# Moving the gates' and picked sums' instructions of six background tails to other steps of a one-core transformer layer

## The reference

```
cluster_gates = _calibrate(xf @ cluster_sigs.T, knots, temperature)     # 8 clusters
cluster_idx   = argmax(cluster_gates)
tile_gates    = _calibrate(xf @ sigs.T, knots, temperature)             # 64 tiles
sel_gates     = the 8 tile gates of the picked cluster
tile_idx      = cluster_idx * 8 + argmax(sel_gates)
...
y = xf + mag(tile_idx) * directions[tile_idx] * output_scale            # then a layer norm
```

## Time and profile before

| | |
|---|---|
| median of 3 runs | 1847.26 us (1846.22 to 1847.81) |
| the profiled execution, its own time | 1845.4 us |
| its span | 1843.6 us |
| TensorE busy | 1751.8 us, 95% of the span |
| VectorE busy | 1158.2 us, 63% |
| ScalarE busy | 1146.2 us, 62% |
| GpSimd busy | 891.7 us, 48% |

### The profile page before, as it was taken

How to read it: one execution, slowest core, us unless ns; L and a number is a source line. 1 busy time by engine, 2 the same in 40 slices (tenths; PEclk the granted TensorE clock), 3 DMA queues, 4 the chain that set the end, 5 groups by cost and what they waited for, 6 DMA issues and landing times.

```text
span 1843.6 us, 27558 instructions
## 1 busy us (share of the span) xinstructions
PE 1751.8 (95%) x9204; PEld 849.1 (46%) x9204; DVE 1158.2 (63%) x2783; ACT 1146.2 (62%) x1554; POOL 891.7 (48%) x811
## 2 busy tenths in 40 slices
PE   5899999999999899999999999999999999999994
PEld 3444454454544445444554445445454444544452
DVE  5465546657476674847657576574756767385767
ACT  3567756666567664666656765666647676566653
POOL 2435535545545454555545354455654555544620
PEclk9899999999999999999999999999999999999997
DMA  5200000100200000010110000001020001000000
GB/s 163 51 13 1 1 12 1 24 13 1 69 1 13 1 12 12 1 35 1 47 24 1 13 1 24 1 1 35 1 58 1 2 1 24 12 1 1 1 12 12
DMA packets 96606, 32.32 MB, mean 18 GB/s; under 512 B 76304, under 2 KB 90704, under 8 KB 96464
## 3 DMA queue, kind: packets, MB, share of 16 engines
q1 hardware_dynamic: 96464, 30.56, 7.9%
HBM read 13.48 MB, written 4.19 MB: 10 GB/s over the span
## 4 chain that ended last, share of the span: by engine, by line
PE 80%; ACT 8%; DVE 7%; issue 4%; POOL 1%; DMA 0%; ACTq 0%; DVEq 0%; SPq 0%; POOLq 0%
PE attended L1295 22%; PE key_scores L1276 21%; PE misc L1205 7%; PE max_scores L1254 6%; PE misc L1335 6%; PE misc L1375 3%; PE misc L1305 3%; ACT relu L1653 2%; ACT probs L1662 2%; PE misc L1366 2%; PE misc L1439 1%; DVE relu L1939 1%; PE misc L1428 1%; PE misc L1210 1%; PE misc L1417 1%
## 5 line engine op out<-in xcount | busy, mean ns | idle before, releaser
L1662 ACT ACTIVATE probs<-key_scores 128x1024 f32<-128x1024 f32 x512 | 524.0, 1023 | 463.7 <-PE key_scores L1276 388.9
L2434 POOL TENSOR_TENSOR prob_sum<-prob_sum,probs 128x512 f32<-128x512 f32 x383 | 491.5, 1283 | 135.7 <-ACT probs L1662 111.7
L1295 PE MATMUL attended<-probs,values 128*64 128x512 f32 x2048 | 556.8, 616 | 0.1
L1939 DVE CUSTOM_DVE_ANT_0 relu<-max_scores,relu 128x512 f32<-128x512 f32 x508 | 330.1, 687 | 258.4 <-PE max_scores L1254 257.4
L1276 PE MATMUL key_scores<-q_high,k_chain 64*128 64x512 f32 x2048 | 459.0, 444 | 17.1 <-ACT probs L1662 16.1
L1276 PEld LDWEIGHTS key_scores<-q_high,k_chain 64*128 64x128 f32 x2048 | 192.2, 184 | 457.4 <-ACT probs L1662 220.6
L1959 DVE TENSOR_TENSOR running_sum<-running_sum,probs 128x512 f32<-128x512 f32 x384 | 266.3, 694 | 10.1 <-ACT probs L1662 3.2
L1653 ACT ACTIVATE relu<-max_scores 128x1024 f32<-128x1024 f32 x254 | 259.0, 1020 | 16.7 <-PE max_scores L1254 10.8
L2430 POOL TENSOR_TENSOR prob_sum<-probs 128x512 f32<-128x512 f32 x64 | 82.0, 1281 | 359.8 <-PE misc L1305 351.8
L1254 PE MATMUL max_scores<-k_max,q_high 64*128 64x512 f32 x1016 | 210.1, 410 | 21.5 <-DVE row_max L1939 13.2
L1276 PE MATMUL key_scores<-q_low,k_chain 64*128 64x512 f32 x1024 | 203.3, 393 | 0.0
(11 more groups left out here) (435 smaller groups left out, 1928.5 us busy)
## 6 DMA issues: line engine op xcount, KB each, us to landing
k_chain<-k_chain SPq DMA_DIRECT2D x32, 256.0 KB, 3.7
shift_row<-row_max SPq DMA_DIRECT2D x512, 0.5 KB, 2.0
buf_a<-in_x SPq DMA_DIRECT2D x8, 512.0 KB, 4.0
k_max<-k_max SPq DMA_DIRECT2D x16, 256.0 KB, 3.4
x_in<-in_x SPq DMA_DIRECT2D x7, 512.0 KB, 4.7
out_x<-buf_b SPq DMA_DIRECT2D x7, 512.0 KB, 3.1
heads_out<-in_qkv_wT SPq DMA_DIRECT2D x1, 1536.0 KB, 10.0
wo<-in_o_wT SPq DMA_DIRECT2D x1, 1024.0 KB, 6.3
```

The costliest lines, as they stand in the source:

```text
L1295: tensor.matmul(attended[head * HD:(head + 1) * HD, :], values_of(b, g // 2)[:, kt, g % 2 * HD:(g % 2 + 1) * HD], prob_slot(u, kt, head), ...
L1662: scalar.activation(probs[(u * KT + kt) % len(probs)][:, :, :], key_scores[:, :, :], ACT.Exp).then_inc(S["exp"])
L1939: vector.tensor_tensor_reduce(out=relu_of(u, i)[:, head, :], in0=max_area(u, i)[:, head, :], in1=relu_of(u, i)[:, head, :], scale=1.0, sca ...
L2434: gpsimd.tensor_tensor(prob_sum[1][:, :], prob_sum[1][:, :], probabilities, ALU.add).then_inc(S["prob_sum1"])
```

## The change

In `calibration`, `cal_b` waits for a step with room, for tails 0 to 5. In `tail`, the GpSimd product `pick_tiles` is put into the same step as the first `first_max`, and `tile_scores`, with the `cal_a` of the second calibration behind it, waits for a step with room, for tails 0 to 5 again (`FIRST_HALF` is 7).

```diff
@@ calibration
     plan.put("cal_a", j, which)
     yield EARLY
     plan.put("cal_exp", j, which)
-    yield LATE
+    yield ROOM if j < FIRST_HALF - 1 else LATE
     plan.put("cal_b", j, which)
```

## The result

| | before | after |
|---|---|---|
| median of 6 runs on one chip | 1847.31 us (1842.73 to 1847.81) | 1852.09 us (1848.78 to 1854.66) |
| after over before | | 1.0034, 95% interval 1.0023 to 1.0044 |
| the profiled execution, its span | 1843.6 us | 1847.0 us |

The kernel became slower, by 0.34% or 6.3 us by the ratio, with 4.2 to 8.1 as its interval (the medians of these few runs differ by 4.8). The prediction was 1847.0 us with a range up to 1851.2 and 0.76 on no change: wrong in sign, and the measured median lies 0.9 us above the range.

The account below looks back on a forecast made before the run. PE, busy 95% of the span, was taken to bound the kernel, so only its waits could shrink. Terms -3.3 - 0.6 - 0.7 + 3.3 + 1.0 = -0.3 us gave 1847.0 us, range 1842.6 to 1851.2.

Parts of the forecast that it names:

- Tails 1 and 3, the wait goes: PE's 1.63 us wait for row maxima in tails 1 and 3 nearly goes, -3.3 us for both.
- Tails 0, 2 and 4, nothing: Moving the picked sums and `cal_a` out of step 114 and its like saves 0, as PE has no wait there.
- preparation of chunks 5 and 7: Preparation moved to step 181 makes PE wait 1.6 us against 1.93 before, twice: -0.6 us, bounds -3.9 and +5.
- First norm: Tails 1, 3, 5, one step later: waits of 1.4 us against 0.36 at steps 140 and 141, three times, +3.3 us.
- Preparation of chunks 4 and 6: Steps 161 to 164: the second norm pair behind `inv` costs 0.6 us against 0.93 before, twice, -0.7 us.
- Tail 5: Second norm to first maximum, two steps later, takes the phase of tail 1: +1.0 us, bounds -1.1 and +2.
- the signs: Expected in the profile after: no `row_max` wait over 0.3 us at steps 177, 305, 431; stated waits at 140, 141, 183.
- GpSimd's queue: `pick_tiles` moves ahead of one running add, which slips about 1.3 us in tails 1 and 3; covered by buffers, 0.
- The port contention: GpSimd instructions lock ports shared with VectorE; so `cal_b` is stretched in chunks 5 and 7's new step, sum -0.3, else -0.9.
- the preparation lands behind GpSimd: Slower rival: `x_stats` starts 2.6 us later, PE waits 4.2; +4.6 for both chunks, 1852.2 us, chance 0.13.
- The later start is free: Faster rival: the losses at the first norm and in tail 5 go, only gains stay; -5.7, 1841.6 us, chance 0.17.
- the change doesn't do what it says: Rival: maxima of step 176 stay late because `first_max` ends late; -3.3 becomes 0, 1850.3 us, chance 0.05.

Follow-up runs that it names:

- e4: The changed kernel, but only the picked sums wait for a step with room, `cal_b` does not; 1847.1 us, ratio 1.0000 to the kernel before.
- e6: The kernel before with `pick_tiles` put with the first maximum in all tails, and tails 1, 3 and 5 started one step later; 1851.9 us, ratio 1.0027.
- e9: The changed kernel with ScalarE's `k_high` of each batch's last half-block of keys one step later; 1850.52 us, ratio 1.0018 to the kernel before.
- e13: e6 with the edit of e9, `k_high` one step later; 1845.2 us, ratio 0.9992 to the kernel before.
- e7: The changed kernel with the preparations of chunks 5 and 7 (and 3) asked for two units later; 1843.95 us, ratio 0.9984 to the kernel before.
- e10: The changed kernel with `pick_tiles` put back behind the wait for a step with room; 1854.28 us, ratio 1.0037 to the kernel before.
- e3: The changed kernel with the waits for room in tails 1 and 3 alone; 1845.87 us, ratio 0.9997 to the kernel before.
- e5: e4 with room for the picked sums in tails 1 and 3 alone; 1839.06 us, ratio 0.9961 to the kernel before.

## Why the prediction was wrong, step by step

**Tails 1 and 3, the wait goes: right.** -1.63 each, the maxima right behind the running sum.

**Tails 0, 2 and 4, nothing: nearly.** No wait came; the stretches are 1.3 us shorter together, by a cause left open. e4 shows the danger there that the step did not name: it weighed `cal_b` only as something that fits between maxima "as it did", and in step 116 it does not.

**A missing step: what the two delays do at steps 133 and 134.** "With tails 1, 3 and 5 one step later" was priced at the first norm only, and `x3` of tails 0, 2 and 4, which goes two steps later with the second calibration, had no term at all. The late start takes a 3.72 us output product from its place between T133 and T134, and that product was the cover of ScalarE's 2.30 us wait for `k_diff`: e6, with nothing but the late start, has 1.57 us of wait there. `x3`, put ahead of the maxima of step 132 and stretched, makes VectorE late: e9 keeps 1.05 us by that alone. 3 times 1.34 = +4.0 us, priced at 0; e13 has neither chain and no wait. The cover's own row was in the trace of before; I had costed the SP queue and the residual's bias at this place, and not asked which long product hid what.

**The term that was furthest off: preparation of chunks 5 and 7, mis-sized, with a wait missed.** -0.6 was predicted, +6.1 measured, 6.7 us off, where the whole sum is 6.5 off; all the rest, the +4.0 above included, nearly cancels. Its start came 3.32 us after T181, not 2.45 to 2.9: GpSimd's four products ran from 0.32 to 2.68, not to 2.2. The way from there to the scores is 4.84, as long as before; the 0.6 taken off it for the absent `q_high` was not to be had. So 2.62 of wait, not 1.6. Then came two things that no term had: 1.35 for the misc bank two steps on, and the lower clock behind the long wait, some 1.2 us in step 183 alone (6.60 against 5.43 in e9 with the same wait) and 1.5 in the stretch. The clock makes 2.9 of the 6.1 us, and not in every execution; without it the term is still +3.2. e7 shows that the place of the preparation is the cause. Which part of the 2.62 is `cal_g`'s and which the step's, no run separates.

**First norm: right in place and in ScalarE's order, too dear.** 1.08 ahead of the scores and the transposes, not 1.4; +2.2 for +3.3. No run changes that order alone; e6 and e13 show that the late start brings the wait.

**Preparation of chunks 4 and 6: too cautious.** The 0.6 that I expected `inv` to leave did not come. -1.9 for -0.7.

**Tail 5: right.** +1.3 beside the waits above, for +1.0; its steps took tail 1's waits one by one, with 0.62 for maxima at step 429, where the signs had named none over 0.3 at 431.

**Tail 6 and GpSimd's queue: a gain not seen.** -0.9 for 0 in tail 6, by a misreading of the diff: the product moves in every tail. Elsewhere too the early product was priced at 0, and against e10 it is worth 0.3 to 0.4 us in each of tails 1, 3 and 5.

**The port contention.** I used the Trainium skill (SBUF — State Buffer, section "SBUF: two separate sides") for `cal_b` only. The rows agree: its third instruction takes 0.93 in the new step (634.69 in the trace after) where it took 0.18, and ends within 0.03 us of GpSimd's add. But the larger effect, of the same kind by its times, is in `x3`, 9.4 us of VectorE's time, and I had not looked for it, because no term had `x3` in another step beside GpSimd's products.

**The rivals.** 1852.2 was given for "the preparation lands behind GpSimd". The time fits and the mechanism does not: that rival needed a start 2 us later with a wait of 4.2, and the start was 0.4 to 0.9 us late. The nearness is a coincidence of sums. "The later start is free" fell with the first norm, and "the change doesn't do what it says" with the maxima of step 176, which are in time.

## What to carry to other kernels

When a piece of a hand-ordered list slips by a step, ask of each long product in it what it was hiding on the other engines, not only what it will wait for itself; a wait of 2.30 us can be in the trace of before and cost nothing until the cover moves. Cost a rule that is applied to all tails for each phase apart: the same move paid 2.9 us in tails 1 and 3 and cost 2.4 in tails 0, 2 and 4, and taking only the places that paid turned +0.34% into -0.39%. Where two late chains meet TensorE at neighbouring places, each hides behind the other's wait and removing either shows little; remove both before calling a cause refuted.

## What the runs showed of the hardware

**A long wait of TensorE may be paid twice, and not always.** In the profiled executions, after the wait of 2.6 us at steps 183 and 311 the work of the step ran slow in both places of the changed kernel (the window above: granted clock 0.53, so near the lower of the two levels, 1.2 of 2.4 GHz), but in neither of e9, whose wait is the same 2.63 us. e9's step 183:

```profile
645.77:651.20 5.43, 2.80 (x19) 1.29 (x17) 4.58 (x18) 4.17 (x8) 3.04 (x4) 1.00 0.03 0
```

The one execution of e3 has both: the wait is 2.58 us at steps 183 and 311, and the step behind each, 184 and 312, takes 3.38 us at a granted clock of 1.00 and 4.50 at 0.73. What decides it, no run shows.

```profile
651.55:654.93 3.38, 3.38 (x23) 1.88 (x22) 1.71 (x5) 2.77 (x4) 2.94 (x3) 1.00 0.00 0
1096.74:1101.24 4.50, 4.50 (x23) 2.19 (x23) 1.50 (x4) 2.31 (x3) 2.54 (x2) 0.73 0.00 0
```

**Step 107, in a stretch that no kernel here changes, takes about 3.75 or 5.3 us.** Some executions have the clock of 1.00 in it and some a lower one; before it, TensorE has waited 1.22, 0.32 and 0.78 us in steps 103 to 106. The same holds for steps 235 and 363, and within one execution too: e3 has 5.35, 3.77 and 3.75 us in the three. The kernel before, then e5:

```profile
391.65:395.40 3.75, 3.75 (x25) 2.36 (x24) 2.51 (x5) 2.10 (x3) 3.52 (x4) 1.00 0.04 0
```

```profile
392.17:397.51 5.34, 5.34 (x26) 2.89 (x25) 2.50 (x5) 2.16 (x3) 3.69 (x4) 0.68 0.03 0
```

That is 1.6 us for each such place, by chance, and such places are a part of the several microseconds by which runs of one kernel differ: of the runs of the kernel before on the chip of e9, that of 1843.11 us has a mean granted clock of 0.989, those of 1850.78 and 1849.74 us have 0.981. Two profiled executions are therefore compared stretch by stretch, not span by span: by spans the change seems to cost 3.4 us, by the stretches from step 113 on 6.3. The stretches still hold what chance does inside them, here 2.9 us.

**`x3` takes longer beside GpSimd's products.** It takes 0.47 to 0.48 us by itself and up to 1.52 beside them (see at steps 133 and 134), and moving it into other steps cost 9.4 us of VectorE's time over 28 instructions.
